# Four gated attention/feed-forward layers: weights of the first two feed-forwards requested earlier, transposes and products alternating by row, another step order in the third attention, one stacked adapter product

## The reference

```python
x = x + tanh(g_xattn[0]) * L0_xattn(ln(x), ctx, ...)   # 32 heads of 128, 4 kv heads, keys = ctx and x
x = x + tanh(g_ffn[0])   * L0_ffn(ln(x), ...)          # base product + 8 adapters, mixed by a softmax over the mean row
x = x + tanh(g_xattn[1]) * L1_xattn(ln(x), ctx, ...)   # 16 heads of 96
x = x + tanh(g_ffn[1])   * L1_ffn(ln(x), ...)          # 8 experts of rank 16, best one per row
x = x + tanh(g_xattn[2]) * L2_xattn(ln(x), ctx, ...)   # 32 heads of 16, 8 kv heads
x = x + tanh(g_ffn[2])   * L2_ffn(ln(x), ...)          # silu(gate) * up, 1376 wide, rank-16 adapters
x = x + tanh(g_xattn[3]) * L3_xattn(ln(x), ctx, ...)   # quantised product
x = x + tanh(g_ffn[3])   * L3_ffn(ln(x), ...)          # block-quantised silu(gate) * up
```

## Time and profile before

| | |
|---|---|
| time, three runs | 1532.28 us median, 1529.94 to 1536.84 |
| the profiled execution's own time | 1530.6 us |
| its span | 1528.9 us |
| PE busy | 1395.6 us, 91% |
| DVE busy | 962.5 us, 63% |
| ACT busy | 596.6 us, 39% |
| POOL busy | 455.6 us, 30% |
| mean granted clock of PE | 0.968 of full speed |

### The profile page before, as it was taken

One profiled execution on the slowest core, in us unless ns is written; L12 is line 12 of the kernel. 1 busy time (PEld: TensorE's weight loads), 2 busy tenths in 40 slices (PEclk: granted clock), 3 DMA queues, 4 the chain that ended last, 5 costly groups with the idle time before them and its releaser, 6 DMA issues.

```text
span 1528.9 us, 22466 instructions
## 1 busy us (share of the span) xinstructions
PE 1395.6 (91%) x8049; PEld 1077.8 (70%) x8049; DVE 962.5 (63%) x1393; ACT 596.6 (39%) x1037; POOL 455.6 (30%) x355
## 2 busy tenths in 40 slices
PE   5999999998999999969999999999798997999765
PEld 4888879887988888834787878878564443666432
DVE  3778557865787578733584848647646763162597
ACT  2444344443444344410443435344255664122121
POOL 2362435243615352421253322421410002143100
PEclk9999999999999999989999999999898999999787
DMA  4110221011201111030011010110220001630000
GB/s 145 56 46 15 60 70 39 22 59 43 60 28 60 42 49 39 12 136 6 22 34 46 4 62 21 31 31 1 84 74 1 2 1 38 157 115 28 0 1 27
DMA packets 53600, 67.41 MB, mean 44 GB/s; under 512 B 26385, under 2 KB 34161, under 8 KB 53505
## 3 DMA queue, kind: packets, MB, share of 16 engines
q1 hardware_dynamic: 53504, 66.12, 14.2%
HBM read 56.41 MB, written 5.37 MB: 40 GB/s over the span
## 4 chain that ended last, share of the span: by engine, by line
PE 80%; DVE 12%; issue 3%; ACT 2%; DMA 2%; POOL 0%; SPq 0%; DVEq 0%; POOLq 0%; ACTq 0%
PE ps L622 12%; PE ps L596 11%; PE ps L534 9%; PE ps L610 8%; PE ps L561 8%; PE ps L554 7%; PE ps L1462 4%; PE ps L1106 2%; PE ps L1475 2%; PE ps L1132 2%; DVE pT L809 2%; PE ps L1467 2%; PE ps L1117 1%; ACT pT L700 1%; PE ps L1088 1%
## 5 line engine op out<-in xcount | busy, mean ns | idle before, releaser
L700 ACT ACTIVATE pT<-ps 128x768 fp32r<-128x768 f32 x192 | 156.0, 812 | 293.6 <-PE ps L610 293.6
L622 PE MATMUL ps<-pT,vv 128*128 128x256 f32 (+1 forms) x1728 | 250.4, 290 | 2.5 <-DVE oT L815 2.5
L809 DVE TENSOR_TENSOR pT<-ps,pT 128x768 fp32r<-128x768 f32 x192 | 183.8, 957 | 93.3 <-ACT pT L700 92.9
L596 PE MATMUL ps<-kT,qT 128*128 128x512 f32 (+3 forms) x1152 | 234.5, 341 | 3.8 <-DVE qT L752 2.4
L596 PEld LDWEIGHTS ps<-kT,qT 128*128 128x128 f32 (+1 forms) x1152 | 200.0, 190 | 43.8 <-DVE qT L752 4.0
L622 PEld LDWEIGHTS ps<-pT,vv 128*128 128x128 f32 (+1 forms) x1728 | 216.2, 181 | 4.3 <-DVE pT L809 2.9
L798 DVE TENSOR_REDUCE nmax<-ps 128x1 f32<-128x768 f32 x192 | 182.3, 951 | 24.9 <-PE ps L596 21.8
L707 ACT ACTIVATE prob<-ps,nmax 128x768 f32<-128x768 f32 x192 | 172.3, 898 | 31.2 <-DVE nmax L798 31.0
L610 PE MATMUL ps<-ident,prob 128*128 128x128 f32 x1152 | 159.4, 275 | 19.5 <-DVE pT L809 19.4
L561 PE MATMUL ps<-wo,oT 128*128 128x512 f32 (+1 forms) x576 | 163.6, 399 | 4.3 <-DVE qT L752 2.6
L610 PEld LDWEIGHTS ps<-ident,prob 128*128 128x128 f32 x1152 | 131.5, 141 | 32.0 <-ACT prob L707 17.5
(11 more groups left out here) (221 smaller groups left out, 1833.3 us busy)
## 6 DMA issues: line engine op xcount, KB each, us to landing
f2raw<-in_f_w SPq DMA_DIRECT2D x11, 776.0 KB, 4.5
w3in<-in_m_w SPq DMA_DIRECT2D x11, 768.0 KB, 4.5
raw<-in_l_wq SPq DMA_DIRECT2D x32, 256.0 KB, 2.7
raw<-in_l_wo SPq DMA_DIRECT2D x32, 256.0 KB, 2.6
raw<-in_l_wq SPq DMA_DIRECT2D x16, 192.0 KB, 2.4
raw<-in_l_wo SPq DMA_DIRECT2D x16, 192.0 KB, 2.4
w3gu<-w3o SPq DMA_DIRECT2D x11, 256.0 KB, 2.6
ctxraw<-in_ctxT SPq DMA_DIRECT2D x2, 1024.0 KB, 7.4
```

The source lines that it names most:

```text
L596: last = nc.tensor.matmul(sc[:, lo:hi], qT[0:hd, h % 2, qp, r * P:(r + 1) * P], kT[0:hd, kp, b, lo:hi], start=(qp, kp) == PAIRS[0], stop=( ...
L622: last = nc.tensor.matmul(bank(6, 256, hd), vv[:, vp, b * VT + j, 0:hd], pT[:, q % 2, pp, j, :], start=(j == 0 and (vp, pp) == PAIRS[0]), ...
L700: nc.scalar.activation(turned_p(m, HI), ps[:, 4:6, 0:S // 2].rearrange("p a (j c) -> p a j c", j=3), ACT.Copy).then_inc(s["pT_hi"], 1)
L809: nc.vector.tensor_tensor(to, ps[:, 4:6, 0:S // 2].rearrange("p a (j c) -> p a j c", j=3), hi, ALU.subtract).then_inc(s["pT"], 1)
```

## The change

- FF 0: `worg`, `fwq` and `fkeys` get SBUF space of their own and are requested early in attention 0; `down` and `up` still wait for `layer_done`. PE goes through transposes and base products by row (`turn_between`), and the small steps of the softmax now stand between base products and parts of the `down` product.
- FF 1: `wa` and `wb` are requested during the last kv head of attention 1; PE alternates transposes and expert products. The output product of the third attention gets the same alternation.
- `layer_done` is raised at the head of the last row's statistics instead of behind them.
- Third attention: in each step one score stands before the turned scores and one behind; the value products come every step instead of in pairs every second; transposes of outputs move from step 2 of a kv head to 3, those of the shifted queries from 3 to 4.
- FF 2: `f2gb` is loaded three times into 96 partitions, POOL makes high, high and low parts of it in float32r (two operations of 2816 columns during the third attention), `f2a` is written three times side by side, DVE subtracts on 32 of the 96 rows of `f2aT`, and the adapter is one float32r product with 96 rows.

```diff
@@ ln_row_variance
             v.wait_ge(counter, value)
+            if r == RT - 1:
+                layer_done(v, counter, value)
...
+        def turn_between(pe, u, work):
+            turn_row(pe, u, 0)
+            for r in range(RT):
+                if r + 1 < RT:
+                    turn_row(pe, u, r + 1)
+                pe.wait_ge(sem("xT_hi"), RT * u + r + 1)
+                work(r)
...
-            over_heads(sp, A, load)
+            over_heads(sp, A, load, (lambda: mlp0_early_sp(sp)) if A is A0 else None)
...
+        def mlp0_early_sp(sp):
+            for dst, name in ((worg, "f0_worg"), (fwq, "f0_wq")):
+                sp.dma_start(dst[:], t[name].rearrange("(k p) n -> p k n", p=P)).then_inc(sem(name), 16)
+            sp.dma_start(fkeys[:], t["f0_keys"]).then_inc(sem("f0_keys"), 16)
...
@@ mlp1_sp
-            sp.wait_ge(sem("layer_done"), 3)
+            sp.wait_ge(sem("att_kv_full"), at(A1.kv - 1, A1, "kv_full", att_per(A1)["kv_full"]))
...
@@ att2_pe, steps
+                m = AHEAD2 + 2 * n
+                if m < G2 * N2:
+                    score(m)
                 turned_score(n)
-                for m in (AHEAD2 + 2 * n, AHEAD2 + 2 * n + 1):
-                    if m < G2 * N2:
-                        score(m)
+                if m + 1 < G2 * N2:
+                    score(m + 1)
...
-                if n and n % 2 == 0:
+                if n >= 2:
                     weighted(n - 2)
-                    weighted(n - 1)
...
@@ mlp2_early_pool
+            nc.gpsimd.tensor_tensor(f2gb3[:].rearrange(flat), f2gb[:].rearrange(flat),
+                                    one[0:96, :].to_broadcast([96, FT * 2 * P]), ALU.mult).then_inc(sem("f2_gb_hi"), 1)
+            g.wait_ge(sem("f2_gb_hi"), 1)
+            nc.gpsimd.tensor_tensor(f2gb3[64:96].rearrange(flat), f2gb[64:96].rearrange(flat),
+                                    f2gb3[64:96].rearrange(flat).bitcast(F32), ALU.subtract).then_inc(sem("f2_gb_lo"), 1)
...
@@ mlp2_pe
-                    nc.tensor.matmul(bank(4 + w), f2gb[:, j, w, :], f2aT[:],
+                    nc.tensor.matmul(bank(4 + w), f2gb3[:, j, w, :], f2aT[:],
                                      start=False, stop=True).then_inc(sem(("f2_gate", "f2_up")[w]), 1)
...
@@ mlp2_dve
+            v.wait_ge(sem("f2_aT"), 1)
+            nc.vector.tensor_tensor(f2aT[32:64, :], ps[32:64, 7, :], f2aT[32:64, :].bitcast(F32),
+                                    ALU.subtract).then_inc(sem("f2_aT_lo"), 1)
...
@@ mlp2_dve, after the last row
-            layer_done(v, sem("added"), 4 * RT)
```

More of the change, by code:

```diff
@@ L272, in build @@
             ctxn = sb("ctxn", [P, 2 * KT, D], F32, grp)
-            f2a = sb("f2a", [P, 2, KT, 32], F32R, grp)
-            f2aT = sb("f2aT", [32, ROWS], F32, grp)
+            f2gb3 = sb("f2gb3", [96, FT, 2, P], F32R, grp)
+            f2a = sb("f2a", [P, 2, KT, 96], F32R, grp)
+            f2aT = sb("f2aT", [96, ROWS], F32R, grp)
             f2db = sb("f2db", [16, D], F32, grp)
@@ L344, in ln_row_dve @@
             if r == RT - 1:
-                layer_done(v, counter, value)
                 ln_row_out(v, s, r)
@@ L360, in build, with turn_row @@
         TURN_BANK = {0: 4, 2: 4, 4: 4}
+        def turn_row(pe, u, r):
+            first = TURN_BANK.get(u, 0)
+            if u == 0 and r == 0:
+                pe.wait_ge(sem("const"), 4)
+            pe.wait_ge(sem("rows_ready"), RT * u + r + 1)
+            for k in range(KT):
+                last = nc.tensor.transpose(ps[:, first + r, k * P:(k + 1) * P], xn[:, r, k * P:(k + 1) * P], ident[:])
+            last.then_inc(sem("turned"), 1)
         def turn_pe(pe, u):
-            first = TURN_BANK.get(u, 0)
             for r in range(RT):
[L365 to L370, removed]
+                turn_row(pe, u, r)
+        def turn_between(pe, u, work):
[5 more added lines that the diff above has]
+                work(r)
         def turn_act(a, u, plain=False):
@@ L864, in base, with down_part, base_and_query @@
                                      start=(k == 0), stop=False)
-            pe.wait_ge(sem("xT_hi"), RT * 2)
-            pe.wait_ge(sem("f0_worg"), 16)
[L868 to L874, removed]
+            def down_part(j):
+                if j == 3:
+                    pe.wait_ge(sem("f0_spread"), 1)
+                for k in range(KT):
+                    last = nc.tensor.matmul(bank(j), down[:, k, j * P:(j + 1) * P], xTf[:, k, :],
+                                            start=(k == 0), stop=(k == KT - 1))
+                last.then_inc(sem("f0_h"), 1)
+            def base_and_query(r):
+                if r == RT - 1:
+                    pe.wait_ge(sem("f0_msum"), 1)
+                    pe.wait_ge(sem("f0_wq"), 16)
+                    for k in range(KT):
+                        last = nc.tensor.matmul(bank(0, B), fwq[:, k, :], msum[:, k, :], start=(k == 0),
+                                                stop=(k == KT - 1))
+                    last.then_inc(sem("f0_small"), 1)
+                base(r)
+            pe.wait_ge(sem("f0_worg"), 16)
+            turn_between(pe, 1, base_and_query)
             pe.wait_ge(sem("f0_qc"), 1)
@@ L887, in mlp0_pe @@
             last.then_inc(sem("f0_small"), 1)
[L888 to L895, removed]
+            down_part(2)
+            down_part(3)
             pe.wait_ge(sem("f0_up"), 16)
@@ L946, in mlp1_pe, with experts @@
         def mlp1_pe(pe):
-            pe.wait_ge(sem("f1_a"), 16)
-            for r in range(RT):
-                pe.wait_ge(sem("xT_hi"), RT * 3 + r + 1)
+            def experts(r):
                 for k in range(KT):
@@ L1177, in att2_pe @@
                         rows(g - 1, "l2_q4", 2 * g + 2)
-                if i == 3 and g + 1 < G2:
+                if i == 4 and g + 1 < G2:
                     if g:
@@ L1194, in att2_out_pe, with out_row @@
         def att2_out_pe(pe):
-            pe.wait_ge(sem("l2_wo"), 16)
-            for r in range(RT):
-                pe.wait_ge(sem("xT_hi"), RT * 5 + r + 1)
+            def out_row(r):
                 for k in range(KT):
@@ L1340, in att2_dve @@
                         shift(m)
-                if i == 2 and g:
+                if i == 3 and g:
                     rows(g - 1)
@@ L1449, in mlp2_pe @@
                 for wp, xp in PAIRS:
-                    last = nc.tensor.matmul(bank(7, 512, 32), f2a[:, wp, k, :], xT[:, xp, k, :],
+                    last = nc.tensor.matmul(bank(7, 512, 96), f2a[:, wp, k, :], xT[:, xp, k, :],
                                             start=(k == 0 and (wp, xp) == PAIRS[0]),
@@ L1517, in mlp2_act @@
             a.wait_ge(sem("layer_done"), 5)
-            nc.scalar.activation(f2a[:, HI], f2a_raw[:], ACT.Copy).then_inc(sem("f2_a_hi"), 1)
+            nc.scalar.activation(thrice(f2a[:, HI]), f2a_raw[:].unsqueeze(2).to_broadcast([P, KT, 3, 32]),
+                                 ACT.Copy).then_inc(sem("f2_a_hi"), 1)
         def mlp2_loop_act(a):
             a.wait_ge(sem("f2_aT_full"), 1)
-            nc.scalar.activation(f2aT[:], bank(7, 512, 32), ACT.Copy).then_inc(sem("f2_aT"), 1)
+            nc.scalar.activation(f2aT[:], bank(7, 512, 96), ACT.Copy).then_inc(sem("f2_aT"), 1)
             def exps(j):
```

49 lines of the change are left out of this document (30 added, 19 removed).

## The result

| | before | after |
|---|---|---|
| time, median of 4 runs, us | 1531.11 | 1491.55 (1490.56 to 1493.64) |
| profiled execution / its span, us | 1530.6 / 1528.9 | 1491.04 / 1489.3 |

What follows compares the result with a forecast made beforehand. PE was taken as the bound, 80% of the chain of waits. Gains of 7.4 (FF 0), -2.5 (FF 1), 3 (third attention), 17.7 and 0.4 (FF 2) and 0.2 made 26.2 us: median 1506, range 1495 to 1515.

Steps and rivals of the forecast that it cites:

- 0.80 saved, 22 times: FF 2's loop: the float32r adapter product saves 0.80 us in each of 22 places, 17.7 us.
- upper bound of 18.5: FF 2's loop: the most the new adapter was expected to gain, 18.5 us, with 12 as the lower bound.
- the new step of 1.54 us: Third attention: score 0.23, turned scores 0.04 + 0.28, last score with passage 0.43, values 0.56; 15.3 us a head.
- every step now has its own passage to value products and back: Third attention: stalls are traded for passages in every step; 0.3 us gained a head, 3 us in the stage.
- 0.56, of which 0.41 idle: Third attention: cost in us of one value step alone, read from a trace row, against 1.00 for two.
- the rival that wins clearly: Third attention: a head takes 13.6 us, 9 us less than forecast in all, time 1497; chance 0.13.
- the slower rival: Third attention: small gaps in every step halve PE's clock, up to 1598 us with all six heads; chance 0.03.
- that rival's 12: Third attention: 12 us gained if the passages overlap, 13.6 us a head; the upper bound of the stage.
- the upper bound of 8: FF 0: the most it was expected to gain, 8 us, around a forecast of 7.4 and a lower bound of 5.
- the 2 us stay: FF 0: some 2 us lost to the half clock at its head remain, as the clock is low there after the change too.
- two rows of transposes: FF 0: transposes now inside the stretch to the up product, 0.6 us each, 1.3 with gaps.
- three more changes between kinds: FF 0: three more changes between kinds of products inside the stretch to the up product, 0.4 us.

Runs made afterwards that it cites:

- Experiment 2: Changed kernel with FF 2's adapter product as float32 on 96 rows, or float32r on 32 rows: the loop took 115.19 and 109.59 us against 101.35.
- Experiment 4: Changed kernel with value products paired again, or both scores behind the turned ones again, in the third attention: 1500.05 and 1494.72 us.
- experiment 5: Changed kernel with FF 0 as before (late weight request, all transposes first), layer_done still early: 1499.95 us.

## Why the prediction was wrong

The direction, the place of every large gain and loss, and FF 1 were right; the time lay below the range. The excess of 13.4 us has three large parts and a smaller one.

**FF 2's loop, 4.6 us.** The term that failed is "0.80 saved, 22 times". It took the old adapter's cost from the start of its product to the start of the next, 1.05. The slot did shrink by that much (1.05 to 0.23), but the same product also lengthened the twelve products beside it, by 0.2 an adapter (the earlier trace rows already show 3.06 for the dozen between two adapters and 2.93 for one that has none ahead of it), and one adapter was worth 1.01. Experiment 2 shows both reasons, type and rows. Its upper bound of 18.5 was worked out from the same slot and so excluded the truth.

**Third attention, 4.1 us.** The step that failed is the new step of 1.54 us, and in it "every step now has its own passage to value products and back", priced from "0.56, of which 0.41 idle" of one late row. That 0.41 is idle time of the weight loads, not of PE: the eight loads of a value block take 0.16, and the next load comes when the block's products are through. It stands behind a pair of value blocks as well, in the kernel before:

```profile
1210.51 0.19 PEld L1117 LDWEIGHTS ps<-q4T,k3T 49*128 49x128 f32 x2 [0.41 <-issue]
```

A value block alone takes 0.57 and two together 1.00, so by these rows a passage of its own costs 0.14, an estimate. And the score, the turned scores and the second score, which the sum had at 0.98 in every step, take that in three of eight steps only and 0.80 in the mean: in the others products on different row halves overlapped though they are of two kinds. So a step, its transposes left out, took 1.41 in the mean instead of 1.54, which times eight is the 1.1 by which a head was shorter than forecast. Experiment 4 shows that the sign of the term was wrong: value blocks in every step gain 0.64 a head over pairs. A head took 14.19, between the forecast (15.3) and the rival that wins clearly (13.6).

On top of this the stage ran at half clock at its first head for 20.5 us in after, 10.2 in the kernel before. This is not what the slower rival had in mind, the small gaps of the new steps: the clock fell at 1140.5, before the first turned scores (1142.42), behind three waits of PE for DVE (0.54, 0.28 and 0.28 us), which the kernel before has too. How long it stayed low differs: 10.2 in both executions of the old order, 10.2, 10.2, 13.7, 17.1, 17.1, 20.5, 20.5 and 20.5 in those of the new one. Whether the new order makes it longer stays open. Where it was 10.2, as in the kernel before, the stage took 111.0 us, 11 less than before, near that rival's 12.

**Start to FF 0, 3.0 us.** Not forecast and, by experiment 5, mostly the clock of single executions. Nothing in the sum failed here; it compared two executions.

**FF 0, 1.7 us.** It gave 8.2 to 9.2 instead of 7.4, over the upper bound of 8. The low clock cost about what the sum had, 1.7 (the first row 5.29, the second 3.60) for "the 2 us stay". What was too dear is "two rows of transposes" with "three more changes between kinds", 1.7 in the sum: a row of transposes between base products takes 0.43 to 0.44 of PE's stream (664.14 to 664.57), 0.9 for two, and the way from the first base product to `up` took 32.73 us instead of the 33.95 worked out. The rest is that the first base product started 0.4 sooner against the transposes than assumed.

Smaller: the output product lost 0.7 by its alternation where 0.2 was forecast as gained. Its first product did start 0.2 sooner; what the sum left out are the transposes of two rows, 0.44 each, that now stand inside the stream. The start of FF 2 gave 0.3 (0.4 forecast), and DVE's wait for `sz` is gone, as forecast.

**FF 1** went as worked out in its mechanism and its size: DVE held at L1006 and L1011 (L979 and L984 before) until POOL's subtractions ended, 2.2 lost (2.5 forecast). One clause was wrong: a DVE operation got in between two POOL operations that left no gap (L1006 ended with the first), but that did not help, since L1011 was then held by the second. The prediction cited the Trainium skill (SBUF — State Buffer, "Who interferes with whom") for a DVE instruction with two SBUF inputs contending with a GpSimd one that reads SBUF. The trace agrees: of the small operations beside the subtractions only the two with two SBUF inputs were held (1.69 and 4.20 us); the reduction between them and the operation with one PSUM input took 0.19 each.

The other rule that it cited from the Trainium skill (TensorEngine Tiling (Array Packing), "Key Properties") is that changing the tiling mode drains TensorE. The 0.41 that the prediction took for its sign was none. A 32-row product in a stream of 128-row ones does cost 0.37 us more than one on 96 rows (experiment 2), which agrees with the rule; that it is a drain no run shows.

The range was too narrow because both bounds of the loop came from one slot, and because the attention's large gain was taken for a rival of 0.13 on the strength of one row that was read as PE's and was not.

## What to carry to other kernels

The price of a foreign product in a dense PE stream is the difference between two whole iterations or two whole blocks, not its own slot: here a fifth of it (0.2 of 1.0) stood in the neighbours. An idle row next to one event is no price for that event unless the trace excludes another cause; idle time of the weight loads, above all, says nothing while PE's products run. Where a small DVE chain lets PE wait, look at what POOL can start beside it once transfers come earlier, and give POOL a wait: it gained more here than the stage had lost.

## What the runs showed of the hardware

- A float32r stream of 512-column products ran at 0.233 us each. One float32 product in it cost a second pass (0.23) and 0.41 in the products behind; 32 rows instead of 96 cost 0.37, half of it in the neighbours. As one float32 product on 32 rows the two cost 1.01, of which 0.2 in the neighbours.
- Ten identity products before the last scores ahead of the third attention's first head, and twelve earlier, kept the granted clock at its upper level where it was at 1.2 GHz for 10 to 20 us in every execution without them. In the changed kernel's trace it had fallen behind waits of PE of 0.54, 0.28 and 0.28 us.
- A DVE operation with two SBUF inputs (0.19 us alone) beside a GpSimd subtraction lasted until that subtraction ended, 1.69 and 4.20 us, and one of them got through between two subtractions that stood back to back.
